# A scan stage's weights prepared one stage earlier, and a stage's first normalisation in four groups of 512 tokens

## What is computed

```python
h = _layernorm(x) * (1 + ca) + sa
x = x + ga * _L0_attn_ref(h, ...)      # 8 heads, rotary, causal
h = _layernorm(x) * (1 + cb) + sb
x = x + gb * _L0_ffn_ref(h, ...)       # tree-routed leaves, 4 networks, attention
h = _layernorm(x) * (1 + ca) + sa
x = x + ga * _L1_attn_ref(h, ...)      # state-space scan
h = _layernorm(x) * (1 + cb) + sb
x = x + gb * _L1_ffn_ref(h, ...)       # 6 layers of local attention and gated hidden layer
```

## Time and profile before

| | us |
|---|---|
| median of three runs | 2866.11 |
| lowest and highest of them | 2861.02, 2868.27 |
| the profiled execution | 2871.75 |
| its span, first to last instruction | 2869.6 |
| PE busy in it | 2485.1 (87%) |
| DVE busy | 2008.9 (70%) |
| ACT busy | 1758.8 (61%) |
| POOL busy | 1468.8 (51%) |

### The profile page before, as it was taken

The page is one execution under the profiler, slowest core; times in us unless marked ns, Lnnn a source line. Parts: engine busy times, 40 slices in busy tenths (PEclk is TensorE's granted clock), DMA queues, the critical chain, the costliest instruction groups (busy, mean ns, idle before and its releaser), DMA issues. The chain is left out here.

```text
span 2869.6 us, 93621 instructions
## 1 busy us (share of the span) xinstructions
PE 2485.1 (87%) x35232; PEld 1697.9 (59%) x35260; DVE 2008.9 (70%) x3074; ACT 1758.8 (61%) x3671; POOL 1468.8 (51%) x1068
## 2 busy tenths in 40 slices
PE   7999758885637777559999999999999999999994
PEld 4777546664423444226666666666667666766663
DVE  5888643223216888558788887888878888788883
ACT  4666513333216777337777777777777777777773
POOL 2444233222123454346666676666766667667660
PEclk9999968998767999779999999999999999999997
DMA  9100015860420000011122111211211111121110
GB/s 332 29 0 0 4 35 164 232 183 25 131 73 1 0 0 0 15 51 28 26 52 49 26 26 48 53 26 26 55 33 38 48 41 26 27 66 33 26 26 28
DMA packets 124764, 149.16 MB, mean 52 GB/s; under 512 B 12144, under 2 KB 111536, under 8 KB 120240
## 3 DMA queue, kind: packets, MB, share of 16 engines
q1 hardware_dynamic: 120592, 139.78, 18.2%
q0 software_dynamic: 4096, 8.40, 1.0%
HBM read 76.83 MB, written 27.26 MB: 36 GB/s over the span
## 5 line engine op out<-in xcount | busy, mean ns | idle before, releaser
L2396 POOL TENSOR_TENSOR c<-a,bq 128x1024 f32<-128x1024 f32 x192 | 455.2, 2371 | 143.6 <-DVE bq L2461 125.9
L2057 PE MATMUL ps<-wqk,xs 128*128 128x512 f32 x768 | 370.1, 604 | 14.7 <-POOL xs L2389 8.7
L2406 POOL TENSOR_TENSOR qn<-c,ss 128x1024 f32<-128x1024 f32 x192 | 365.4, 1903 | 28.4 <-issue 3.4
L2460 DVE TENSOR_TENSOR a<-ps,tab 128x512 f32<-128x512 f32 x384 | 263.1, 685 | 80.4 <-ACT sq L2233 77.2
L2233 ACT ACTIVATE sq<-ps 128x512 f32<-128x512 f32 x384 | 224.4, 597 | 94.8 <-PE ps L2057 60.4
L2461 DVE TENSOR_TENSOR bq<-ps,tab 128x512 f32<-128x512 f32 x384 | 261.5, 681 | 0.0
L1459 POOL TENSOR_TENSOR hC<-hs,Cs 128x1024 f32<-128x1024 f32 x64 | 150.3, 2353 | 191.2 <-ACT Cs L1610 105.2
L2414 POOL TENSOR_TENSOR z<-z,sm 128x1024 f32<-128x1024 f32 x96 | 182.8, 1904 | 109.6 <-DVE sm L2489 98.8
L2468 DVE TENSOR_REDUCE ss<-sq 128x16 f32<-128x1024 f32 x192 | 230.3, 1200 | 3.9 <-POOL qn L2406 2.5
L2068 PEld LDWEIGHTS ps<-ident,qn 128*128 128x128 f32 x1536 | 172.6, 141 | 76.8 <-POOL qn L2406 41.5
L2068 PE MATMUL ps<-ident,qn 128*128 128x128 f32 x1536 | 205.5, 277 | 4.3 <-POOL qn L2406 2.8
(11 more groups left out here) (313 smaller groups left out, 5782.6 us busy)
## 6 DMA issues: line engine op xcount, KB each, us to landing
Ve<-Vo SPq DMA_DIRECT2D x96, 256.0 KB, 4.3
Ve<-Vo SPq DMA_DIRECT2D x96, 192.0 KB, 4.4
win_rows<-rows_q SPq DMA_DIRECT2D x24, 256.0 KB
outs_q<-win_out SPq DMA_DIRECT2D x24, 256.0 KB
wqk<-in_wqkv SPq DMA_DIRECT2D x6, 1024.0 KB, 5.0
leaves<-in_f_w SPq DMA_DIRECT2D x9, 576.0 KB
leaves<-in_q_w SPq DMA_DIRECT2D x1, 4608.0 KB, 18.8
leaves<-in_k_w SPq DMA_DIRECT2D x1, 4608.0 KB, 22.7
```

The costliest lines, as they stand in the source:

```text
L2057: nc.tensor.matmul(jobs.out(n), xs[:, t * 128:(t + 1) * 128], wqk[:, (2 * y + s) * 512:(2 * y + s + 1) * 512], start=True, stop=True).then ...
L2396: nc.gpsimd.tensor_tensor(f(c), f(a), f(bq), ALU.add).then_inc(c_ready.sem, 1)
L2406: nc.gpsimd.tensor_tensor(qn[:, t, y, :, :, :].rearrange("p h s e -> p h (s e)"), c[:, y, :, :, :].rearrange("p h s e -> p h (s e)"), spre ...
L2460: nc.vector.tensor_tensor(a[:, y, :, s, :], Zs, spread(table(0, s), H1), ALU.mult)
```

## The change

The scan stage's weights get a class of their own, allocated before the routed stage and kept to the scan stage's end. Their ten loads are issued by SP at the routed stage's start; the decay rates are made by ACT at that stage's end, the cast and the tap products by DVE after its last step and before it waits for the transposed outputs. `sel` shrinks to 96x32 elements, and the cast repeats each one 128 times as it reads. The taps are multiplied in place. In the scan stage the loads, the three waits for them and the preparations are gone.

The local stage's first normalisation is written out for four groups of 512 tokens, each with its own PSUM banks and its own part of three large tiles that the main loop needs only later. The six DMAs of layer 0's weights stand behind the three loads in that first block, and DVE casts the mask at its end. The class `Norm` is gone.

```diff
@@ routed0, SP
                 sp.dma_start(kst[:, :], d["rank"]).then_inc(kl, 16)
+                core.scan_weights.load(core, sp)
@@ routed0, ACT
                 act.preload_act_table_set("natural_log_exp_and_others")
+                core.scan_weights.decay_rates(core, act)
@@ routed0, DVE
                     step(t, S1, S1 + WG)
+                core.scan_weights.taps_and_rows(core, dve)
                 for g in range(NG4):
                     dve.wait_ge(*filled(f"FT{g}"))
@@ new
+    def load(self, core, sp):
+        d = core.dram
+        for dst, n in ((self.win[:, :], "win"), (self.wx[:, :, :], "wx"), (self.wdt[:, :], "wdt"), (self.wout[:, :, :], "wout"),
+                       (self.taps[:, :, :].rearrange("p k c -> p (k c)"), "convw"), (self.cb[:, :], "convb"), (self.bdt[:, :], "bdt"),
+                       (self.A[:, :, :], "A_log"), (self.Dp[:, :], "Dp"), (self.sel[:, :], "sel")):
+            sp.dma_start(dst, d[n]).then_inc(self.loads, 16)
+
+    def decay_rates(self, core, act):
+        rates = self.A[:, :, :].rearrange("p k n -> p (k n)")
+        act.wait_ge(self.loads, 160)
+        core.nc.scalar.activation(rates, rates, ACT.Exp)
+        act.drain()
+        core.nc.scalar.activation(rates, rates, ACT.Copy, scale=-1.0)
+        act.drain()
+
+    def taps_and_rows(self, core, dve):
+        dve.wait_ge(self.loads, 160)
+        core.nc.vector.tensor_copy(self.sel_b[:, :].rearrange("p (n c) -> p n c", c=128), spread(self.sel[:, :], 128, 2))
+        for j in range(KC):
+            core.nc.vector.tensor_tensor(self.taps[:, j, :], self.win[:, 0:DI], self.taps[:, j, :], ALU.mult)
+        dve.drain()
@@ mamba1
-            @block.sync
-            def _(sp):
...
-                    sp.dma_start(dst, d[n]).then_inc(loads, 16)
-                sp.wait_ge(loads, 160)
...
-                pe.wait_ge(loads, 160)
...
-                act.wait_ge(loads, 160)
...
-                nc.scalar.activation(flat(A[:, :, :]), flat(A[:, :, :]), ACT.Exp)
...
-                dve.wait_ge(loads, 160)
-                nc.vector.tensor_copy(sel_b[:, :], sel[:, :])
-                for j in range(KC):
-                    nc.vector.tensor_tensor(wtap[:, j, :], win[:, 0:DI], cw[:, j * DI:(j + 1) * DI], ALU.mult)
-                dve.drain()
@@ local1, first block
+        m_cent, m_lsq, m_lrs = (t[:, :, :, :, :].rearrange("p y h s e -> p (y h s e)") for t in (a, bq, c))
+        jobs0 = Jobs(core.banks, [(f"{n}{g}", 4 * j + g, 1) for j, n in enumerate(("mean", "var")) for g in range(NG4)], 1)
@@ SP
+                load_front(sp, row_of(0))
+                load_values(sp, row_of(0))
+                load_mid(sp, row_of(0))
+                load_hidden(sp, row_of(0))
+                load_late(sp, row_of(0))
                 sp.wait_ge(loads, 48)
@@ PE
-                with pe.Fori(0, NB) as b:
-                    norm0.pe_mean(pe, b, x[:, cols(b)])
-                    norm0.pe_var(pe, b, 1)
+                for g in range(NG4):
+                    pe.wait_ge(*jobs0.free(0, f"mean{g}"))
+                    nc.tensor.matmul(jobs0.out(f"mean{g}"), core.mean_w[:, :], x[:, c512(g)], start=True, stop=True)\
+                        .then_inc(jobs0.sem_filled(f"mean{g}"), 1)
+                for g in range(NG4):
+                    pe.wait_ge(*jobs0.free(0, f"var{g}"))
+                    pe.wait_ge(m_squared, g + 1)
+                    nc.tensor.matmul(jobs0.out(f"var{g}"), core.mean_w[:, :], m_lsq[:, c512(g)], start=True, stop=True)\
+                        .then_inc(jobs0.sem_filled(f"var{g}"), 1)
@@ ACT
-                with act.Fori(0, NB) as b:
-                    norm0.act_root(act, b, 1)
+                for g in range(NG4):
+                    act.wait_ge(m_centered, g + 1)
+                    nc.scalar.activation(m_lsq[:, c512(g)], m_cent[:, c512(g)], ACT.Square).then_inc(m_squared, 1)
+                for g in range(NG4):
+                    root = m_lrs[:, c512(g)]
+                    act.wait_ge(*jobs0.filled(0, f"var{g}"))
+                    nc.scalar.activation(root, jobs0.out(f"var{g}"), ACT.Ln, bias=core.eps[:, EPS_LN:EPS_LN + 1])\
+                        .then_inc(jobs0.sem_drained(f"var{g}"), 1)
+                    act.drain()
+                    nc.scalar.activation(root, root, ACT.Exp, scale=-0.5).then_inc(m_scaled, 1)
@@ DVE
-                dve.wait_ge(loads, 48)
-                nc.vector.tensor_copy(wmask_b[:, :, :], spread(wmask[:, :], 8))
+                for g in range(NG4):
+                    dve.wait_ge(*jobs0.filled(0, f"mean{g}"))
+                    nc.vector.tensor_tensor(m_cent[:, c512(g)], x[:, c512(g)], jobs0.out(f"mean{g}"), ALU.subtract)\
+                        .then_inc(jobs0.sem_drained(f"mean{g}"), 1)
+                    dve.drain()
+                    dve.sem_inc(m_centered, 1)
                 for p in (0, 64):
                     for q in (0, 64):
                         nc.vector.tensor_copy(ident_b[p:p + 64, q:q + 64], core.ident[p:p + 64, p:p + 64])
...
+                for g in range(NG4):
+                    dve.wait_ge(m_scaled, g + 1)
+                    nc.vector.tensor_tensor(m_cent[:, c512(g)], m_cent[:, c512(g)], m_lrs[:, c512(g)], ALU.mult)
+                    dve.drain()
+                    for b in (2 * g, 2 * g + 1):
+                        for rows, out in halves(b):
+                            nc.vector.tensor_scalar(out, m_cent[rows, b * T:(b + 1) * T], core.mod[1][rows, 4, b:b + 1],
+                                                    core.mod[1][rows, 3, b:b + 1], ALU.mult, ALU.add)
+                dve.wait_ge(loads, 48)
+                nc.vector.tensor_copy(wmask_b[:, :, :], spread(wmask[:, :], 8))
+                dve.drain()
```

More of the change, by code:

```diff
@@ L114 @@
 EPS_VALUES = (LN_EPS, 1e-6, 1e-5, 0.5 * math.log(2.0 ** 16), 1.0, 1e-36)
[L117 to L144, removed]
-        dve.drain()
[L146 to L150, removed]
-    def act_root(self, act, it, k, sample=False):
-        self.act_square(act, it, k)
-        self.act_rsqrt(act, it, sample)
-    def act_rsqrt(self, act, it, sample=False):
-        nc, eps = self.c.nc, self.c.eps
-        act.wait_ge(*self.jobs.filled(it, self.name + "var"))
-        out = self.jobs.out(self.name + "var")[:, 0:T]
-        if sample:
-            act.wait_ge(self.c.one, 1)
-            nc.scalar.activation(self.rs[:, :], out, ACT.Ln, scale=D / (D - 1.0), bias=self.c.tiny[:, 0:1])
-            act.drain()
-            nc.scalar.activation(self.rs[:, :], self.rs[:, :], ACT.Exp, scale=0.5)
-            act.drain()
-            nc.scalar.activation(self.rs[:, :], self.rs[:, :], ACT.Ln, bias=eps[:, EPS_TINY:EPS_TINY + 1])
-        else:
-            nc.scalar.activation(self.rs[:, :], out, ACT.Ln, bias=eps[:, EPS_LN:EPS_LN + 1])
-        act.drain()
-        last = nc.scalar.activation(self.rs[:, :], self.rs[:, :], ACT.Exp, scale=-0.5)
-        last.then_inc(self.jobs.sem_drained(self.name + "var"), 1)
-        act.drain()
-        act.sem_inc(self.scaled.sem, 1)
@@ L1396, in mamba1 @@
         dBx = core.banks.ps[:, 0:2, :]
-        loads = core.sem("l1a_loads")
         S = lambda n, per, credit=0: Count(core.sem("l1a_" + n), per, credit)
@@ L1591, in _ @@
                 act.preload_act_table_set("natural_log_exp_and_others")
-                nc.scalar.activation(flat(A[:, :, :]), flat(A[:, :, :]), ACT.Exp)
-                act.drain()
-                nc.scalar.activation(flat(A[:, :, :]), flat(A[:, :, :]), ACT.Copy, scale=-1.0)
-                act.drain()
                 def decay(b, g, dt):
@@ L2009, in layer @@
                             sp.wait_ge(wo_used, l * NB)
-                            load_mid(here)
+                            load_mid(sp, here)
                             weights_here(wo_loaded, l * 16 + 16, mid_ok)
@@ L2597, in build @@
         core = Core(nc, ctx, dram)
-        with ExitStack() as early:
-            core.routed = Routed(core, early)
-            for stage in STAGES:
-                if stage in (attention0, routed0):
-                    stage(core)
-        for stage in STAGES:
-            if stage not in (attention0, routed0):
-                stage(core)
+        with ExitStack() as ahead:
+            core.scan_weights = ScanWeights(core, ahead)
+            with ExitStack() as early:
+                core.routed = Routed(core, early)
+                attention0(core)
+                routed0(core)
+            mamba1(core)
+        local1(core)
         store(core, out)
```

81 lines of the change are left out of this document (34 added, 47 removed).

## The result

The changed kernel takes 2823.82 us (median of four runs, 2821.34 to 2827.14), the kernel before beside it 2863.65 us (four runs, 2861.02 to 2868.27). The ratio is 0.9859 with a 95% interval of 0.9843 to 0.9874, so 40 us less. The forecast was 2820.9 us in a range of 2813 to 2829.

What follows compares the result with a forecast made beforehand. The local stage's first normalisation was taken as a chain of waits, the scan start as a wait for loads, ahead of a TensorE-bound loop; 15.6 + 29.6 = 45.2 us off the 2866.11 us median gave 2820.9 us, range 2813 to 2829.

Steps and rivals of the forecast that it cites:

- The two terms of the sum: Savings at the scan stage's start, 15.6 us, and in the local stage's first normalisation, 29.6 us; together 45.2 us.
- if the time between the table products and the end, 1630 us, changes: One of three stated signs of being wrong: the local stage's time after its table products was to stay 1630 us.
- a held gather: End of the routed stage: up to 6.0 us in the range's upper end, for moved VectorE work delaying GpSimd's gather.
- Scan start: Start of the scan stage: without loads, cast and products, centring comes at 843.85 instead of 859.47, 15.6 us less.
- The routed stage's new work: Routed stage: load issues, cast, products and two ScalarE operations hide in idle time and cost zero.
- Rival (a): End of the routed stage: VectorE's cast and products hold the gather, up to 6.0 us later, 2826.9 us; chance 0.07.
- Local normalisation: Local stage's start: four groups of 512 bring table products to 1209.75 from 1239.35, 29.6 us less (28.0 to 32.0).
- Early weights: Local stage's first block: calling for layer 0's weights there gains zero, since the first projection still waits for the tokens.
- The loop's 1630 us: Local stage's main loop: the time from table products to the end stays 1630 us, so nothing is added.
- Nothing of the loop's code or its first wait changes: Local stage's main loop: the reason given for a chance of only 0.03 that the loop loses TensorE's clock.
- Rival (c): Local stage's main loop loses TensorE's clock: 2.8 points cancel the 45 us, at 0.95 some 65 us lost; chance 0.03.
- Base: The starting time of the forecast for the whole kernel: 2866.11 us, the median of three runs of the kernel before.

Runs made afterwards that it cites:

- when forced: Changed kernel with VectorE's moved cast done four times and made to run beside the last gather's indirect DMAs: 2825.62 us against 2862.98, ratio 0.9875.
- the second comparison: The changed kernel and the kernel before, both unchanged, measured again side by side: 2830.67 us against 2874.36, ratio 0.984.
- +1 instruction: The kernel before with only the local stage's part of the change, one more wait on TensorE ahead of the loop: 2849.9 us, ratio 0.9905.
- +17: Changed kernel with four more 512-column matmuls on TensorE while VectorE makes the tables: 2818.66 us, ratio 0.9847 to the kernel before.
- +33: Changed kernel with 8 more 32-column matmuls in TensorE's wait for the routed stage's last gather: 2825.63 us, ratio 0.9879 to the kernel before.
- +241: Changed kernel with 60 more 32-column matmuls in TensorE's wait for the routed stage's last gather: 2818.76 us, ratio 0.9855 to the kernel before.

## Why the prediction was right

The two terms of the sum were right in mechanism and nearly in size; the loop, put at nothing, was not, and by the prediction's own sign ("if the time between the table products and the end, 1630 us, changes") it was wrong there. That the total still came out 2.9 us from the forecast is in part luck: a base 2.5 us too high and two terms 1.5 us too small stood against a loss of some 6 us that the sum has at nothing. And the range holds the result only by the 6.0 us that it has for a held gather, which did not happen; without them its upper end is 2823.0.

- **Scan start, 15.6 us.** Measured 15.8 to 16.0 in every profile with this part (17.09 to 17.24 down to 1.27 to 1.31). TensorE's first matmul ran 0.04 us after the stage's start, not 0.38, which is the missing 0.3 us. ScalarE had its table at 833.67, ahead of the centred tokens at 833.86. By the 2.7 us that the Trainium skill states for a load with its drain (ScalarE: Activation LUTs, "Step-by-step: what each stage is for") it would have been ready at 835.1, 1.2 us after them; the load took 1.28 us again, and ScalarE's next operation started at 833.90.
- **The routed stage's new work, 0.** Right: 29.24 us from gather to end, as before. The gap from the products' end to the gather was 11.4 us, not 7: the 7 was for a cast of twice the time, which it did not take (9.7 us with 2.29), and VectorE's last step ended 1.6 us further ahead of the gather. Rival (a) did not occur, but its mechanism is real, at 6.7 us when forced; its price for one cast would be 2.3 and not 6.0.
- **Local normalisation, 29.6 us (28.0 to 32.0).** Measured 30.8, and 32.4 where the burst began at the full clock. Scaling began 8.17 us after the stage's start, not 9.18: the first matmul ran at 0.05 us and not at 0.38, the burst was let up sooner (eight records took 5.37 us where I had 5.65), and from its end to the first root were 1.34 us and not 1.7. A group cost 2.48 us against 2.46.
- **Early weights, 0.** Right, by the wait on the tokens that stands in both versions.
- **The loop's 1630 us.** This is the step that failed. "Nothing of the loop's code or its first wait changes" was true of the code and not of its place: the written-out normalisation shifted TensorE's instructions ahead of the loop, and a stand for fetched instructions moved from where a wait hid it into line 2107, at both ends of the loop. Against the mean of 1630.8 us with the old normalisation the loop took 1.2 to 10.9 us more, 6.0 in the mean of five profiles. The stand and the lower clock behind it are shown for the third interval, 1.3 to 5.0 us of it; that all of the loss comes from such stands is argued and not shown. Rival (c) named the right object, the loop's clock, but a steady loss; this one comes only at the ends.
- **Base.** The kernel before ran at 2863.65 us in the comparison, 2.5 less than the median I started from.

With measured terms: 15.9 + 30.8 - 6.0 = 40.7 us, against 40 measured (36 to 45 by the interval) and 46 in the second comparison (42 to 50), which lies above the sum; what gave it the rest is open.

## What to carry to other kernels

A chain of small rounds through single buffers at a stage's start is worth writing out in large groups; what it costs can be read off beforehand from a stage of the same kernel that already has that shape. Work moved for an idle engine should be placed by what it slows beside it (here a cast beside indirect DMAs), not by that engine's idleness alone. And adding or removing code ahead of a tight loop can move a stand on issue within it: compare the gaps marked as issue with the packets of the instruction queues, and the first and last passes, not only the steady one.

## What the runs showed of the hardware that I had not expected

- A stand of TensorE on issue, 0.7 to 2.1 us, moves with the number of instructions ahead of it, two to a matmul record (+1 instruction: 6 to 7 records left; +17: 14; +33: 22), and goes from a line with +241. It ends 2.2 to 2.9 us after a 16,384-byte packet of an instruction queue started. Neither is seen in the loop's steady passes.
- TensorE's clock left the full level within 2.70 us in which it was busy for 0.36, in one profile of the changed kernel, and stayed up in another with 0.37. Over the whole run-out, stands of 1.6 us and more go with 109 to 113 us, smaller ones or none with 105 to 107; the cause of that is not shown.
- Casts on VectorE stretch an indirect DMA of GpSimd's from 0.97 to 4.21 us; products of two operands beside one leave it at 0.95.
- A cast that reads each element 128 times is as fast as one that reads 4096 different ones, 2.29 us.
- The rest of the scan stage took 328.4 us in three profiles and 330.2 to 333.3 in the others; the cause is open.
